# Moving the moments of two layer norms from GpSimd to VectorE, in the steps of a graph, LSTM and diffusion kernel

## The reference

```python
def _layernorm(x, axis=-1, eps=1e-05):
    m = jnp.mean(x, axis=axis, keepdims=True)
    v = jnp.var(x, axis=axis, keepdims=True)
    return (x - m) / jnp.sqrt(v + eps)
...
    x = _layernorm(x + _L0_gnn_ref(...))
    x = _layernorm(x + _L1_gnn_ref(...))
    x = _layernorm(x + _L2_gnn_ref(...))
    x = _layernorm(x + _L3_gnn_ref(...))
```

## Time and profile before

| | us |
|---|---|
| median of 3 runs | 998.44 (998.06 to 1000.43) |
| the profiled execution | 999.66 |
| its span | 997.7 |
| TensorE busy | 912.7 (91%) |
| VectorE busy | 648.7 (65%) |
| ScalarE busy | 578.3 (58%) |
| GpSimd busy | 309.7 (31%) |

### The profile page before, as it was taken

The page is one execution under the profiler, slowest core; times in us unless marked ns, Lnnn a source line. Parts: engine busy times, 40 slices in busy tenths (PEclk is TensorE's granted clock), DMA queues, the critical chain, the costliest instruction groups (busy, mean ns, idle before and its releaser), DMA issues.

```text
span 997.7 us, 14843 instructions
## 1 busy us (share of the span) xinstructions
PE 912.7 (91%) x5034; PEld 790.2 (79%) x5034; DVE 648.7 (65%) x1554; ACT 578.3 (58%) x1292; POOL 309.7 (31%) x555
## 2 busy tenths in 40 slices
PE   6799996957999799999999999999999999999695
PEld 4688884446888479988998998898899899888584
DVE  6689994766577665576667667666666765755522
ACT  5366755742564457467657746755774684575331
POOL 3666551032210322144126215303521620230412
PEclk9799997978999989999999999999999999999897
DMA  5322101310100110101201010110110001001000
GB/s 174 117 75 64 68 28 42 148 55 9 32 1 12 42 33 11 43 1 43 64 1 43 28 38 11 33 64 1 43 64 1 12 22 33 1 11 33 1 22 22
DMA packets 26595, 38.55 MB, mean 39 GB/s; under 512 B 3333, under 2 KB 12422, under 8 KB 26010
## 3 DMA queue, kind: packets, MB, share of 16 engines
q1 hardware_dynamic: 26088, 36.05, 10.8%
q10 hardware_dynamic: 434, 1.57, 0.5%
HBM read 21.89 MB, written 15.73 MB: 38 GB/s over the span
## 4 chain that ended last, share of the span: by engine, by line
PE 57%; POOL 7%; DVE 7%; ACT 5%; issue 2%; ACTq 0%; DMA 0%; SPq 0%; POOLq 0%; DVEq 0%
PE psum L136 16%; PE psum L138 16%; PE psum L137 16%; PE psum L1707 2%; PE psum L1708 2%; PE psum L1711 2%; POOL x_rstd L1187 1%; ACT x L1276 1%; POOL out_rstd L1187 1%; ACT raw L1341 1%; POOL node_l L1197 1%; ACT gate L1245 1%; DVE x_stats L1434 1%; DVE nat_l L1579 1%; DVE tl L1482 1%
## 5 line engine op out<-in xcount | busy, mean ns | idle before, releaser
L1245 ACT ACTIVATE gate<-psum,gate_bias 128x256 f32<-128x256 f32 (+2 forms) x296 | 144.4, 559 | 88.0 <-PE psum L1711 70.2
L136 PE MATMUL psum<-in_h,wih_h 128*128 128x256 f32 (+2 forms) x312 | 108.0, 346 | 8.7 <-DVE in_l L1428 6.4
L137 PE MATMUL psum<-in_l,wih_h 128*128 128x256 f32 (+2 forms) x312 | 104.4, 335 | 0.0
L138 PE MATMUL psum<-in_h,wih_l 128*128 128x256 f32 (+2 forms) x312 | 104.3, 334 | 0.0
L1409 DVE TENSOR_TENSOR gate<-gate 128x256 f32<-128x256 f32 (+2 forms) x48 | 23.9, 499 | 93.3 <-ACT gate L1245 93.2
L1211 POOL TENSOR_TENSOR gate<-in_h,in_l 128x512 f32<-128x512 f32 x16 | 20.5, 1304 | 185.0 <-DVE in_l L1428 185.0
L136 PEld LDWEIGHTS psum<-in_h,wih_h 128*128 128x128 f32 x312 | 59.9, 192 | 20.5 <-DVE in_l L1428 9.9
L136 PE MATMUL psum<-e_h,th 128*128 128x384 f32 x180 | 62.6, 348 | 5.1 <-DVE tl L1482 3.3
L1248 ACT ACTIVATE gate<-cell 128x512 f32<-128x512 f32 (+2 forms) x80 | 40.2, 503 | 43.0 <-DVE cell L1412 35.2
L137 PEld LDWEIGHTS psum<-in_l,wih_h 128*128 128x128 f32 x312 | 60.0, 192 | 5.0 <-issue 0.2
L138 PEld LDWEIGHTS psum<-in_h,wih_l 128*128 128x128 f32 x312 | 60.0, 192 | 4.8
(11 more groups left out here) (368 smaller groups left out, 2939.9 us busy)
## 6 DMA issues: line engine op xcount, KB each, us to landing
x_spill<-x SPq DMA_DIRECT2D x30, 256.0 KB, 2.0
xt<-in_x_t_dram SPq DMA_DIRECT2D x16, 256.0 KB, 2.7
raw<-x_spill SPq DMA_DIRECT2D x16, 256.0 KB, 2.9
o_spill<-xt SPq DMA_DIRECT2D x14, 256.0 KB, 2.0
xt<-o_spill SPq DMA_DIRECT2D x14, 256.0 KB, 3.2
x<-x_spill SPq DMA_DIRECT2D x14, 256.0 KB, 3.4
out_dram<-raw SPq DMA_DIRECT2D x14, 256.0 KB, 2.3
raw<-in_adj_t_dram ACTq DMA_DIRECT2D x1, 1024.0 KB, 8.9
```

The lines of the kernel that those rows point to most:

```text
L136: pe.matmul(dst, lh, rh, start=start, stop=False, **kw)
L137: pe.matmul(dst, lh, rl, start=False, stop=False, **kw)
L138: return pe.matmul(dst, ll, rh, start=False, stop=stop, **kw)
L1245: nc.scalar.activation(gate[q][:, 0:n], banks[GATE_BANK[q]][:, 0:n], ACT.Tanh if q == 2 else ACT.Sigmoid, bias=gate_bias[:, p - 1, q:q + 1 ...
```

## The change

In the roots of x2 and x3 GpSimd no longer forms the moments: a new function power_of does the power and the shift only, for GpSimd's turn, x3sum and x3first. VectorE's turn and x3sum (and x3first) call spread_of in place of stats_of: behind the four statistics it forms mean, gap, variance and the sum of the last two in seven instructions, with three waits on itself, and then signals GpSimd. In turn, VectorE waits for x2_ready of the pair before in place of x2_shift. The output norm keeps root and stats_of.

```diff
+            def power_of(norm, asked, shifted, count):
+
+                pool.wait_ge(asked, count)
+                chain.link(nc.gpsimd.tensor_tensor(norm.rstd[:], norm.rstd[:], exponent[:, 0:norm.tiles], ALU.pow))
+                nc.gpsimd.tensor_tensor(norm.shift[:], norm.mv[:, 0, :], norm.rstd[:], ALU.mult).then_inc(shifted, 1)
+
             def turn(g, j):
-                root(x2_norm[j], x2_asked, x2_shift, GB * g + j + 1)
+                power_of(x2_norm[j], x2_asked, x2_shift, GB * g + j + 1)
...
             def x3sum(g, j):
-                root(x3_norm[j], x3_asked, x3_shift, GB * g + j + 1)
+                power_of(x3_norm[j], x3_asked, x3_shift, GB * g + j + 1)
...
+            def spread_of(norm, tiles, asked):
+
+                for i, ap in enumerate(tiles):
+                    ins = nc.vector.bn_stats(norm.stats[:, i, :], ap)
+                chain.link(ins)
+                even, odd = norm.stats[:, :, 0:3], norm.stats[:, :, 3:6]
+                mean, gap, var = (norm.mv[:, i, :] for i in range(3))
+                nc.vector.tensor_tensor(mean, even[:, :, 1], odd[:, :, 1], ALU.add)
+                nc.vector.tensor_tensor(gap, even[:, :, 1], odd[:, :, 1], ALU.subtract)
+                chain.link(nc.vector.tensor_tensor(var, even[:, :, 2], odd[:, :, 2], ALU.add))
+                nc.vector.tensor_scalar(mean, mean, -0.5, None, ALU.mult)
+                nc.vector.tensor_scalar(var, var, 1.0 / D, EPS, ALU.mult, ALU.add)
+                chain.link(nc.vector.scalar_tensor_tensor(out=gap, in0=gap, scalar=0.25, in1=gap, op0=ALU.mult, op1=ALU.mult))
+                nc.vector.tensor_tensor(norm.rstd[:], gap, var, ALU.add).then_inc(asked, 1)
+
             def turn(g, j):
...
-                need(dve, x2_shift, n + 1 - GB)
-                stats_of(x2_norm[j], [x2[j][:, t, :] for t in range(NT)], x2_asked)
+                need(dve, x2_ready, n + 1 - GB)
+                spread_of(x2_norm[j], [x2[j][:, t, :] for t in range(NT)], x2_asked)
...
-                stats_of(x3_norm[j], [x3[:, j, t, :] for t in range(NT)], x3_asked)
+                spread_of(x3_norm[j], [x3[:, j, t, :] for t in range(NT)], x3_asked)
```

## The result

The changed kernel takes 1010.26 us (median of 4 runs, 1008.59 to 1012.35), the kernel before 999.23 us beside it (998.06 to 1000.43): ratio 1.0111, 95% interval 1.0086 to 1.0136. Forecast were 1000.7 us and a range up to 1005.5, so both are wrong. The profiled execution took 1012.35 us for a span of 1010.4, 12.7 more than the span before.

What follows compares the result with a forecast made beforehand. TensorE was taken as the bound, busy 83.97 of 85.20 us a step. Terms -1.7 + 2.7 + 3.8 + 0.4 - 2.9 = +2.3 us on the median 998.44 gave 1000.7 us, range 996.8 to 1005.5.

Steps and rivals of the forecast that it cites:

- steps 2 to 6: The five equal steps: output shift and coefficient products 0.75 us later in each, +3.8 us in all (bounds 3.0 and 5.5).
- step 7: Step without x2 norm or node_l: output shift 1 to 1.8 us later, mostly hidden by TensorE's low clock; +0.4 us.
- The moved norm: Each of 32 norms costs VectorE 0.92 us of queue; the power starts 1.0 us behind the statistics.
- node_l 5.4 us behind those statistics: In steps 2 to 6 GpSimd's low half comes 5.4 us behind the end of x2's statistics, where it was 7.4.
- No idle time at in_l: In steps 2 to 6 TensorE's 0.46 us wait for the LSTM input vanishes, but into a longer wait for tl.
- The bias products' 7.9: In steps 0 and 1 TensorE idles 7.9 us before the bias products instead of 6.11.
- The tail's 3.3 to 3.7: TensorE's hole before the last image's transposes shrinks to 3.3 to 3.7 us from 6.20; -2.9 us.
- The start: Before the steps (g = -1), TensorE's wait for GpSimd's node_l shortens: -1.7 us (bounds -0.9 and -2.0).
- The clock: Slower rival: the idle piece before the coefficient products lowers TensorE's clock, 1.7 us a fall, 1009 if all five; chance 0.18.
- Steps 0 and 1: VectorE's longer queue delays TensorE's square by 0.9 us and its bias products by 1.8 us: together +2.7 us.
- no collision: Rival: x3sum_1's moments are not held by node_l, so +0.1 us per step, 997.5 us in all; chance 0.20.
- the shorter root wins: Faster rival: the saved 1.8 us reaches the output root, each step gives all 1.2 us idle, 990.9 us; chance 0.10.

Runs made afterwards that it cites:

- again: The changed kernel as it is, profiled and measured a second time beside other kernels: 1011.04 us, ratio 1.0110 to the kernel before.
- out_first: The changed kernel, but in the steps VectorE takes the output norm's statistics ahead of image 1's x3 norm: 988.69 us, ratio 0.9894 to the kernel before.
- x2_only: The changed kernel with the x3 norms as before on both engines, only x2's moments on VectorE: 992.83 us, ratio 0.9943 to the kernel before.
- extra_bn: Kernel with only x2's moments moved, plus four extra statistics instructions and one self-wait behind each x3 norm's statistics: 1001.93 us, ratio 1.0033.
- pad: The changed kernel with nine unread matmuls in TensorE's queue ahead of the coefficient products, steps 1 to 6: 1005.87 us, ratio 1.0067.

## Why the prediction was wrong

The profiled span grew by 12.7 us where the sum had 2.3. Of the 10.4 between them 5.7 lie in steps 2 to 6 (the root and the clock) and 4.35 in step 7; 2.5 lie in the first half and are not the change's, and the other stages give 2.2 back.

**The mechanism was right, and so were its steps up to the root.** The moved norm: cell 2 starts 0.81 behind the end of x2's statistics (617.66 to 618.47); against the 0.08 ahead of the end of the earlier trace rows that is 0.89 us of queue, predicted 0.92. node_l 5.4 us behind those statistics: 5.36. The first moment of x3 over 1 us and ending with node_l: 1.05. No idle time at in_l: none. The root of the output norm 8.2 us behind cell 2 (621.2 - 612.98): 8.19. The bias products' 7.9: 7.94. The tail's 3.3 to 3.7: 3.63, and -3.0 for -2.9. The start came out 2.7 shorter where 1.7 was said, in part by luck: the product that waits for node_l starts 1.45 us sooner (1.53 in "again"), since 2.17 us less idle time there is paid in part with 0.89 us for VectorE's L1572 ahead of it, a wait that the step had put at nothing. The rest is the clock: 1.00 over 223 to 226, where the kernel before has 0.57 over 222 to 226.

**Mis-sized in a step of 2 to 6: the root itself.** The step said that the root's overlaps change places and put the output shift at 626.6, 5.4 us behind the root's start and 0.75 later than before. The root took 6.00, and the step grew by 1.18 us instead of 0.75. How long it runs goes with where VectorE's cell 3 meets it: 4.85 us in out_first (cell 3 starts 1.7 behind it), 5.45 in x2_only (1.1 behind), 5.22 in the kernel before (0.8), 5.88 in extra_bn (0.3), 6.00 here, where cell 3 starts 0.16 ahead of it, the root's first instruction takes 1.18 and its power 2.03. No run moves cell 3 alone, so this cause is read from traces and not tested. Even the upper bound, +1.1 per step, was passed. From x2_only to the changed kernel a step (without clock) grows by 2.3 us: 0.9 for the moments' own place in the queue, 0.9 for the hold, 0.55 for the longer root.

**The clock was a rival at 0.18 and should have been part of the forecast.** It was priced at 1.7 us a fall and tied to a hole near 2.1 us. The hole became 2.42 (its 1.8 plus the root's error), and two of five steps fell, at 1.5 each: 3.0 us. Its place was right and its price nearly so.

**Step 7 (+0.4 forecast, +4.75 measured) is the largest miss.** The step said that TensorE's low clock behind the first hole hides most of a later output shift. The shift comes 6.0 us behind out_stats instead of 4.8, and 0.9 of queue ahead of that, 2.1 in all where 1 to 1.8 was said. And the cover was not there: between the holes the clock was 1.00 (0.57 behind the first hole in the earlier trace rows), so TensorE was through early and stood idle for 1.88 us. The clock fell only then, was 0.50 over the next 5.8 us, and fell once more behind the third hole, of which the prediction had read in the earlier trace rows that 1.8 us idle left it at 1.00.

**Steps 0 and 1.** The two waits grew as said, by 0.86 and 1.83 us. What no step foresaw is the clock. In step 0 it was 0.66 over 263 to 273, 0.83 before, which cost 1.4 us more. In step 1 2.1 us came back: 0.6 behind the bias products, where the full clock returned sooner, and 1.5 by a fall that the kernel before has (first row) and the changed one has not (second row):

```profile
372.20:377.00 4.80, 4.78 (x19) 4.80 (x20) 2.24 (x6) 2.64 (x8) 0.00 (x0) 0.64 0.00 0
...
375.60:379.00 3.40, 3.40 (x21) 3.40 (x22) 2.04 (x6) 2.78 (x9) 0.00 (x0) 1.00 0.00 0
```

The rivals "no collision" and "the shorter root wins" are refuted for this kernel; the second is what happens once the order is changed. Two slips in the prediction's sums change nothing: without the steps they come to -1.5 and not -1.4, and the in_l hole is 0.46 in the earlier trace rows where the clock's rival adds 0.41.

## What to carry to other kernels

When work is moved to another engine's queue, look at what stands behind it there at the moment that the moved work's own result sets free: the gain (node_l 2.0 us sooner behind x2's statistics) and the loss (out_stats later) were both right in size, and one exchange in the queue's order kept the first without the second. Test halves of a change apart and together; here they do not add up, by 15 us. Where a change makes a hole of TensorE's longer, price the clock with it: here a fall cost 1.5 us behind a hole of 2.4 us, and in step 7, with a second hole behind the first, 3.7 us.

## What the runs showed of the hardware

- A VectorE tensor_scalar with one SBUF input (128x4) is held by a GpSimd subtraction as long as a tensor_tensor is (1.06 us both, elsewhere 0.17); bn_stats beside the same subtraction is not (four in 0.85 us).
- Equal holes do not fall alike. Behind a hole of 2.40 to 2.45 us in steps 2 to 6 TensorE's clock fell in 13 of 25 cases over five profiles (2, 2, 3, 3, 3), behind one of 1.5 us in none of 5. The Trainium skill ("TensorE: Matmul & The Clock Gate", Part 1) ties the clock to how busy the array has been lately. The trace of pad agrees: with the hole filled but for 0.4 us no step fell. Which of two equal holes is followed by a fall is explained by no trace here and stays open.
- TensorE's busy time is no floor for a step: it was 83.97 of 85.20 us, from which the prediction took 1.2 us as the most that a step can give. out_first gives 1.7: its period is 83.53 us, of which 83.39 are busy. Part of the difference is seen: behind each of the two holes the first product takes 0.28 us to the next one's start, in out_first 0.17, and the profile counts that as busy.
